# Cross-attention and ternary FFN on one core: the high halves of the FFN's passes as fp16 beside fp32r low halves

## The reference, cut to what matters

```python
x = x + xattn(layernorm(x), ctx)          # softmax(q k^T) v Wo, per batch of 256 rows
n = layernorm(x)                          # no gains
def bitlinear(x, w):                      # w is replaced by sign-like values in {-1, 0, 1}
    scale = clip(mean(abs(w), axis=1), 1e-5)
    tern = clip(round(w / scale), -1, 1)
    return x @ (tern * scale).T
h = bitlinear(n, w_fc) + gate * (n @ v.T @ fast_b.T @ u.T)    # 512 -> 2048, rank 16
r = max(h, 0)
x = x + bitlinear(r * r, w_proj)          # 2048 -> 512
```

## Time and profile before

| what | value |
|---|---|
| median of 3 runs | 780.21 us (779.91 to 780.46) |
| the profiled execution | 779.99 us, its span 778.2 us |
| TensorE busy (PE) | 766.5 us, 98% |
| weight loads (PEld) | 637.6 us, 82%, beside PE |
| VectorE (DVE) | 547.6 us, 70% |
| ScalarE (ACT) | 368.6 us, 47% |
| GpSimd (POOL) | 107.4 us, 14% |
| granted TensorE clock | 1.00 of full speed over the span |

### The profile page before, as it was taken

How to read it: one execution, slowest core, us unless ns; L and a number is a source line. 1 busy time by engine, 2 the same in 40 slices (tenths; PEclk the granted TensorE clock), 3 DMA queues, 4 the chain that set the end, 5 groups by cost and what they waited for, 6 DMA issues and landing times.

```text
span 778.2 us, 10596 instructions
## 1 busy us (share of the span) xinstructions
PE 766.5 (98%) x3767; PEld 637.6 (82%) x3767; DVE 547.6 (70%) x1118; ACT 368.6 (47%) x690; POOL 107.4 (14%) x125
## 2 busy tenths in 40 slices
PE   7999999999999999999999999999999999999997
PEld 4678788888888888888888888888888888888886
DVE  5999766778676777667766786768667686656434
ACT  5998744354434535354434545254542644233332
POOL 3101300100211030110312020210202002100001
PEclk9999999999999999999999999999999999999999
DMA  8743431163115322063214422063212430040101
GB/s 315 248 150 109 63 88 41 21 96 87 56 40 84 58 72 85 13 97 69 81 42 65 65 75 96 1 99 70 90 41 41 75 88 1 1 54 9 47 0 55
DMA packets 180125, 56.20 MB, mean 72 GB/s; under 512 B 167620, under 2 KB 167894, under 8 KB 180072
## 3 DMA queue, kind: packets, MB, share of 16 engines
q1 hardware_dynamic: 149940, 50.79, 26.8%
q10 hardware_dynamic: 30132, 4.73, 3.8%
HBM read 26.92 MB, written 8.39 MB: 45 GB/s over the span
## 4 chain that ended last, share of the span: by engine, by line
PE 97%; DVE 1%; ACT 1%; issue 0%; DMA 0%; DVEq 0%; ACTq 0%
PE H L1357 30%; PE O L1338 29%; PE G L1220 26%; PE H L1363 4%; PE H L1220 1%; PE H L1197 1%; PE H L1204 1%; PE O L1412 1%; PE G L1304 1%; PE O L1378 1%; PE H L1185 1%; PE G L1248 0%; DMA Wq_s<-in_L_xattn_Wq_dram 0%; DVE x2a L1057 0%; PE O L1395 0%
## 5 line engine op out<-in xcount | busy, mean ns | idle before, releaser
L1338 PE MATMUL O<-projT,qbuf 128*128 128x512 f32 x992 | 242.1, 390 | 0.0
L1338 PEld LDWEIGHTS O<-projT,qbuf 128*128 128x128 f32 x992 | 185.0, 188 | 38.2
L779 ACT ACTIVATE rbuf<-H,scf 128x512 f32<-128x512 f32 x128 | 87.5, 684 | 124.9 <-DVE qbuf L1116 75.7
L1357 PE MATMUL H<-even_group,fcT 128*128 128x512 f32 x512 | 127.5, 391 | 0.0
L1357 PE MATMUL H<-odd_group,fcT 128*128 128x512 f32 x512 | 127.3, 391 | 0.0
L1112 DVE TENSOR_TENSOR rbuf<-rbuf 128x512 f32<-128x512 f32 x128 | 91.5, 723 | 45.9 <-ACT rbuf L779 45.9
L787 ACT ACTIVATE qbuf<-rbuf 128x512 fp32r<-128x512 f32 x125 | 78.5, 628 | 89.7 <-PE O L1338 62.7
L1116 DVE TENSOR_TENSOR qbuf<-rbuf,qbuf 128x512 fp32r<-128x512 f32 x125 | 85.9, 688 | 36.5 <-ACT qbuf L787 35.8
L1357 PEld LDWEIGHTS H<-odd_group,fcT 128*128 128x128 f32 x512 | 95.3, 188 | 19.3
L1357 PEld LDWEIGHTS H<-even_group,fcT 128*128 128x128 f32 x512 | 95.1, 188 | 19.2
L1220 PE MATMUL G<-Wvo,tT 128*128 128x512 f32 x270 | 64.7, 389 | 0.0
(11 more groups left out here) (194 smaller groups left out, 989.0 us busy)
## 6 DMA issues: line engine op xcount, KB each, us to landing
xb<-in_x_dram SPq DMA_DIRECT2D x8, 1024.0 KB, 5.1
n_blocks<-n_rows SPq DMA_DIRECT2D x112, 64.0 KB, 2.3
ctxb<-in_ctx_dram SPq DMA_DIRECT2D x8, 768.0 KB, 4.3
n_blocks<-ctxb SPq DMA_DIRECT2D x112, 48.0 KB, 2.2
wring<-in_L_ffn_w_fc_dram SPq DMA_DIRECT2D x16, 256.0 KB, 6.2
wring<-in_L_ffn_w_proj_dram SPq DMA_DIRECT2D x16, 256.0 KB, 2.7
out_dram<-x2a SPq DMA_DIRECT2D x8, 512.0 KB, 2.7
x_blocks<-x_rows SPq DMA_DIRECT2D x56, 64.0 KB, 3.5
```

The source lines that it names most:

```text
L779: nc.scalar.activation(rbuf[:, j % 2, :], banks[f"H{j % 2}"][:, :], ACT.Relu, scale=scf[:, j:j + 1]).then_inc(relu_made, 1)
L1338: mm = pe.matmul(banks[f"O{t}"][:, :], qbuf[:, j % 2, h, t * P:(t + 1) * P], projT[:, j, :], start=(j == 0 and h == HI), stop=(j == NFF - ...
L1357: pe.matmul(banks[f"H{j % 2}"][:, :], fcT[:, k, j * P:(j + 1) * P], xnT[:, h, k, :], start=(k == 0 and h == HI), stop=False)
```

## The change

1. The high halves of the FFN's input and of the squares are fp16 tiles (`hi16_of`, `square_hi`; for the last pieces `late_square_hi`). The weights of their passes are the same ternary tiles, read as bf16 through every second 2-byte element (`fc16`, `pc16`). Low halves, the low-rank pass and the attention stay fp32r.
2. `up` and `down` do the four passes of one half, then the four of the other. They begin with the half of the kind that came last (`latest`): fp16 when the piece before ended with high halves, else fp32r. After a piece of the attention it is the fp32r kind. The low-rank pass goes with the low half. A `down` that begins with low halves waits for `lo:j` at its start, one that begins with high halves waits for `hi:j` there and for `lo:j` four passes later.
3. `L:0` still wants fp32r high halves: GpSimd copies them (`x32:0` to `x32:3`, once in each body, and twice as many half-size copies in the prologue).
4. So that squares fit fp16, the scale of the hidden rows is divided by a power of two that comes from a bound made on the chip in the prologue: GpSimd's `peaks`, `power`, `bound`, `rescale`; VectorE's `widest`, `q:0`, `q:1`, `root`; TensorE's `q:0`, `q:1`.
5. Orders: in BODY_ORDER and LAST_ORDER two `down` follow two `up`; at the start of body 0 `up:0` and `up:1` are cut into `main` and `rank`, with `L:0` behind `main:0`; in BODY_ORDER `xhi3` goes ahead of `nc1+` and `xraw3` ahead of `lo:14`.

```diff
 BODY_ORDER "pe":
-        "up:12 down:9 up:13 down:10 up:14 down:11 up:15 down:12 down:13 "
+        "down:9 up:12 up:13 down:10 down:11 up:14 up:15 down:12 down:13 "
 BODY_ORDER "act":
-        "hi:11 up:12 nc0+ xhi0 up:13 xhi1 xhi2 hi:12 hi:13 up:14 up:15 hi:14 nc1+ nc2+ hi:15 xhi3 nc3+ "
+        "hi:11 up:12 nc0+ xhi0 up:13 xhi1 xhi2 hi:12 hi:13 up:14 up:15 hi:14 xhi3 nc1+ hi:15 nc2+ nc3+ "
 BODY_ORDER "dve":
-        "sq:14 sq:15 lo:14 xraw3 xlo3 lo:15 "
+        "sq:14 sq:15 xraw3 lo:14 xlo3 lo:15 "
 BODY_ORDER and FIRST_ORDER "pool":
-        "residual xs23+ a:0 a:1 a:2 a:3 cs23+ "
+        "residual xs23+ a:0 a:1 a:2 a:3 cs23+ x32:0 x32:1 x32:2 x32:3 "
 LAST_ORDER "pe":
-        "... up:2 down:0 up:3 down:1 up:4 down:2 ... down:9 up:12 down:10 up:13 up:14 up:15 down:11 "
+        "... up:2 up:3 down:0 down:1 up:4 up:5 down:2 down:3 ... down:9 up:12 up:13 down:10 up:14 up:15 down:11 "
 PROLOGUE "pe":
-        "... s:3 ut:0 ut:1 ut:2 turn:22 pT:1 w:0 ... x:3 sprow B.L:0 B.up:0 B.up:1 B.up:2 turn:31 "
+        "... s:3 q:0 ut:0 ut:1 ut:2 turn:22 q:1 pT:1 w:0 ... x:3 sprow B.main:0 B.L:0 B.main:1 B.rank:0 turn:31 B.rank:1 B.up:2 "
 PROLOGUE "dve":
-        "... round:25 pT:0 s:3 abs:31 n2:3 round:26 round:27 pT:1 B.xs01 B.xs23 w:0 ... B.cs23 B.L:0 B.sq:0 round:31 B.lo:0 ..."
+        "... round:25 widest pT:0 s:3 q:0 abs:31 n2:3 round:26 round:27 q:1 pT:1 B.xs01 B.xs23 root w:0 ... B.cs23 round:31 B.L:0 B.sq:0 B.lo:0 ..."
+        fc16 = fcT[:, :, :].bitcast(BF16).rearrange("p k (n h) -> p k n h", h=2)[:, :, :, 1]
+        pc16 = projT[:, :, :].bitcast(BF16).rearrange("p n (d h) -> p n d h", h=2)[:, :, :, 1]
 # GpSimd, a step x32:k of a body
+            pool.wait_ge(xhi_made, KD * b + k + 1)
+            nc.gpsimd.tensor_copy(xhi32(g, k), hi16_of[g % 2][:, k, :]).then_inc(xhi32_made, 1)
 # TensorE
             def down(b, j):
-                pe.wait_ge(sqlo_made, NFF * b + j + 1)
+                pe.wait_ge(sqhi_made, NFF * b + j + 1)
-                for t in range(TILES):
-                    for h in (HI, LO):
-                        mm = pe.matmul(banks[f"O{t}"][:, :], qbuf[:, j % 2, h, t * P:(t + 1) * P], projT[:, j, :],
-                                       start=(j == 0 and h == HI), stop=(j == NFF - 1 and h == LO))
-                mm.then_inc(down_full, 1)
+                halves = order_of_halves()
+                for h in halves:
+                    if h == LO:
+                        pe.wait_ge(sqlo_made, NFF * b + j + 1)
+                    for t in range(TILES):
+                        latest["pass"] = pe.matmul(
+                            banks[f"O{t}"][:, :], squares(b, j)[h][:, t * P:(t + 1) * P], (pc16, projT)[h][:, j, :],
+                            start=(j == 0 and h == halves[0]), stop=(j == NFF - 1 and h == halves[1]))
+                latest["half"] = halves[1]
+                done(down_full)
+            def up_half(b, j, h, start, stop):
+                for k in range(KD):
+                    ternary = (fc16 if h == HI else fcT)[:, k, j * P:(j + 1) * P]
+                    tokens = hi16_of[b % 2][:, k, :] if h == HI else group_of[b % 2][:, LO, k, :]
+                    latest["pass"] = pe.matmul(banks[f"H{j % 2}"][:, :], ternary, tokens,
+                                               start=(start and k == 0), stop=(stop and k == KD - 1))
+                latest["half"] = h
 # a step "up": halves = order_of_halves() if kind == "up" and j > 0 else (HI, LO)
```

More of the change, by code:

```diff
@@ L34 @@
 F32R = mybir.dt.float32r
+I32 = mybir.dt.int32
 BF16 = mybir.dt.bfloat16
@@ L47 @@
 FIRST_LATE = NFF - 3
+CREST = 60.0
 ATTENTION = ([("n1T", t) for t in range(4)] + [("n2T", t) for t in range(4)]
@@ L74, in on_act @@
 def on_act(unit):
-    return unit[0] != "a"
+    return unit[0] not in ("a", "q")
 def n_full(b, unit):
@@ L93, in bank_of @@
 def bank_of(b, unit):
-    n = unit_list(b).index(unit)
+    if unit[0] == "q":
+        return f"{'GH'[unit[1]]}0"
+    n = [u for u in unit_list(b) if u not in RANGE].index(unit)
     if b >= 0:
@@ L383, in mk_xattn_ffn @@
         raw_of[0] = under("even_halves", [P, 2, KD, TOK])
+        hi16_of[0] = under("even_hi16", [P, KD, TOK], FP16)
         even = sb("even_group", [P, 2, KD, TOK], F32R)
@@ L386, in mk_xattn_ffn @@
         rbuf = sb("rbuf", [P, 2, TOK])
-        qbuf = sb("qbuf", [P, 2, 2, TOK], F32R)
+        square_hi = sb("square_hi", [P, 2, TOK], FP16)
+        square_lo = sb("square_lo", [P, 2, TOK], F32R)
+        sb("below_x2b", [P, 512])
         x2b = sb("x2b", [P, TILES, D])
+        peaks = sb("peaks_of_squares", [P, NFF, RK])
+        pair = sb("pair_of_peaks", [P, 2, NFF])
+        power = sb("power_of_FB", [P, KD, 16])
+        widest = sb("widest", [P, 2])
+        crest = sb("crest", [P, 4])
+        bound = sb("bound", [P, 2])
+        root = sb("root", [P, 2])
+        scf2 = sb("scf_of_scaled_squares", [P, NFF])
+        spc2 = sb("spc_of_scaled_squares", [P, KD])
+        fsq = sb("power_of_FB_rows", [P, 1])
         x2 = [x2a, x2b]
@@ L943, in unit @@
                     return
+                if kind == "q":
+                    dve.wait_ge(unit_full, n_full(b, un))
+                    if t == 0:
+                        link(nc.vector.tensor_reduce(crest[0:2, 3:4], bank[0:2, 0:P], AX_X, ALU.max))
+                        nc.vector.tensor_scalar(root[0:2, :], ident[0:2, 0:2], crest[0:2, 3:4], None, ALU.mult
+                                                ).then_inc(unit_dve, 1)
+                    else:
+                        nc.vector.tensor_copy(crest[:, 0:3], bank[:, 0:3]).then_inc(unit_dve, 1)
+                    return
                 if kind == "a":
@@ L1135, in steps @@
                                                 ALU.add, apply_absolute_value=True).then_inc(abs_by_dve, 1)
+                    elif kind == "root":
+                        dve.wait_ge(bound_made, 1)
+                        link(nc.vector.tensor_scalar(root[:, 0:1].bitcast(I32), bound[:, 1:2].bitcast(I32), 0x7F800000, None,
+                                                     ALU.bitwise_and))
+                        nc.vector.reciprocal(root[:, 1:2], root[:, 0:1]).then_inc(root_made, 1)
+                    elif kind == "widest":
+                        dve.wait_ge(peaks_made, 1)
+                        nc.vector.tensor_reduce(widest[:, :], pair[:, :, :], AX_X, ALU.max).then_inc(widest_made, 1)
                     elif kind == "uprep":
@@ L1257, in unit @@
                     else:
-                        pe.wait_ge(xhi_made, KD * b)
-                        products(bank[:, :], [(FB[:, k, :], xnT[:, HI, k, :]) for k in range(KD)], last=False)
+                        products(bank[:, :], highs, last=False)
                         pe.wait_ge(xlo_made, KD * b)
@@ L1325, in turn_free, with order_of_halves, done @@
                     piece_stored(pe, j - 4)
+            latest = {"pass": None, "half": LO}
+            def order_of_halves():
+                return (latest["half"], 1 - latest["half"])
+            def done(full):
+                latest["pass"].then_inc(full, 1)
             def down(b, j):
-                pe.wait_ge(sqlo_made, NFF * b + j + 1)
+                pe.wait_ge(sqhi_made, NFF * b + j + 1)
                 if j == 0:
@@ L1408, in _ @@
             for t in range(TILES):
-                for j in range(NFF - 4, NFF):
-                    pe.wait_ge(sqlo_made, NFF * (NG - 1) + j + 1)
-                    for h in (HI, LO):
-                        mm = pe.matmul(banks[f"O{t}"][:, :], squares(NG - 1, j)[:, h, t * P:(t + 1) * P], projT[:, j, :],
-                                       start=False, stop=(j == NFF - 1 and h == LO))
-                mm.then_inc(down_full, 1)
+                halves = order_of_halves() if t > 0 else (HI, LO)
+                for h in halves:
+                    for j in range(NFF - 4, NFF):
+                        pe.wait_ge((sqhi_made, sqlo_made)[h], NFF * (NG - 1) + j + 1)
+                        latest["pass"] = pe.matmul(
+                            banks[f"O{t}"][:, :], squares(NG - 1, j)[h][:, t * P:(t + 1) * P], (pc16, projT)[h][:, j, :],
+                            start=False, stop=(j == NFF - 1 and h == halves[1]))
+                latest["half"] = halves[1]
+                done(down_full)
 _INS = ['x', 'ctx_768', 'L0_xattn_ln1_g', 'L0_xattn_ln1_b', 'L0_xattn_ln2_g', 'L0_xattn_ln2_b', 'L0_xattn_Wq',
```

166 lines of the change are left out of this document (126 added, 40 removed), and 12 rows, old and new, of the table PROLOGUE.

## The result

| | before | after |
|---|---|---|
| median of the runs | 780.34 us (779.91 to 780.46, 4 runs) | 791.53 us (790.92 to 792.22, 4 runs) |
| ratio | | 1.0146, interval 1.013 to 1.0162 |
| profiled execution, its span | 779.99 us, 778.2 us | 791.44 us, 789.6 us |

The change makes the kernel slower by 11.2 us. The forecast was 780.5 us, its range ended at 788.0: wrong in size and outside the range. The nearest case was rival 3's 791.0 us, which was given 0.07; as will be seen, it holds for one half of its passes only, and the rest of the time comes from elsewhere.

The account below looks back on a forecast made before the run. TensorE, busy for 98% of the span, was taken to bound the kernel. The terms -10.5 + 2.3 + 6.4 + 1.4 + 0.7 = +0.3 us on 779.99 us led to a forecast of 780.5 us, range 774.0 to 788.0.

Parts of the forecast that it names:

- rival 3: The fp16 passes are no faster, as weights at every second element or mixed types cost 10.3 ns: 791.0 us, chance 0.07.
- Part 1: In up and down, 1024 high-half passes become fp16, each 10.3 ns shorter than fp32r: -10.5 us.
- Part 2: On TensorE, 163 changes of kind to fp16 and as many back, 14 ns a pair: +2.3 us.
- Part 3: In bodies 1 to 5, down:9, moved ahead of up:12, waits 1.27 us for lo:9: +6.4 us.
- Parts 4 and 5: Start of body 0: up:2 and up:3 wait for the relu, +1.4 us; prologue: VectorE's steps for the bound, +0.7 us.
- the excursion of 104 ns at 91.64: Kernel before, 91.64 to 93.78 us: fp16 and fp32r passes take 104 ns over due; upper bound on changes, 17.0 us.
- Rival 1: At changes of kind, the fp32r load waits for the fp16 passes, up to 104 ns each: 795.2 us, chance 0.22.
- Rival 2: The wait at down:9 in bodies 1 to 5 doesn't come: 774.1 us, chance 0.15.
- Part 6: Splitting into fp16 on ScalarE and VectorE, and GpSimd's copies in the bodies (widest operation 1.55 us), cost nothing.

Follow-up runs that it names:

- e1: The changed kernel with the high-half passes of down moving packed 2-byte elements of projT in place of every second one (wrong numbers): 786.44 us.
- e2: The changed kernel with the high-half passes of up moving every second 2-byte element in place of the packed fp16 tile (wrong numbers): 796.75 us, a single execution.
- e5: The kernel of e4 with high and low halves alternating pass by pass in every up and down, 128 pairs of changes a body instead of 32: 798.4 us.
- e3: The changed kernel with lo:9 moved right behind lo:8, ahead of sq:10 and cs23+, in VectorE's order of bodies 1 to 6: 785.78 us.
- e4: The kernel of e3 with every up and down beginning with its high halves, 32 pairs of changes a body instead of 21: 785.42 us.
- e6: The kernel of e4 with the start of body 0 in the order before the change: 783.92 us.
- e7: The kernel of e6 without the bound of the squares and all that makes it, the power of two being the constant 1: 783.02 us.
- f3: The kernel of e4 with the whole FFN in 16 bits, packed bf16 weights, no GpSimd copies, and body 0 started in the order before: 757.05 us.
- f1: The kernel of e4 with the FFN in 16 bits, packed bf16 weights and no GpSimd copies, but low-rank tiles and passes in fp32r: 763.74 us.

## Why the prediction was wrong, by its own steps

| step | forecast, us | found, us |
|---|---|---|
| Part 1, fp16 passes | -10.5 | -5.7 (`up`, 512 x 11.2 ns), -0.4 (`down`, 512 x 0.7 ns) |
| Part 2, changes of kind | +2.3 | +2.6 (163 x 16 ns, at the change itself) |
| nothing in the forecast: the fp32r passes behind a change | 0 | +3.7 (0.48 a body, 7.75 bodies' worth) |
| Part 3, `down:9` | +6.4 | +6.8 (5 x 1.36) |
| Parts 4 and 5, start and prologue | +2.1 | +4.3 (3.33 + 0.94 in the table of bodies) |
| sum | +0.3 | +11.3, of 11.45 in the profiled executions |

Of the 11.0 us between the two sums Part 1 holds 4.4, the changes with the passes behind them 4.0, the start 2.2 and `down:9` 0.4. That the measured time lies beside rival 3's 791.0 us is chance: of that rival's 10.5 us only 4.4 came.

**Part 1 failed in one sentence:** "Reading one half of each 4-byte weight takes no more bytes per column than today's read, so I price it at nothing". It is right for weights that are loaded (`up`) and wrong for weights that move (`down`), where the step of 4 bytes costs all of the gain. The bound stood beside it, no faster than fp32r, and rival 3 named the mechanism ("weights at every second element"); but I treated both products alike, though the code shows that `projT` is the moving operand of `down` and `fcT` the loaded one of `up`. e1 and e2 show it: 0.58 us less and 0.57 more in body 6, -5.1 and +5.2 us in all. The estimate of 216.4 ns for a packed pass was good; 215.5 was measured.

**Part 2** was right on the change itself (14 ns forecast, 15 in the records of after), and "Behind a 216 ns pass it is hidden, and I take 0" holds up within some 4 ns. What failed is the step behind it, which took every remaining fp32r pass at today's 226.7 ns. They came out at 224 to 239, so that a pair costs 38 ns in after. The prediction's own rows bear it: the excursion of 104 ns at 91.64 has, behind its first fp32r pass, five more at 228 to 236 ns in the records, but only the first was read, and the rest went into a bound. Rival 1 (104 ns a pair, an fp32r load that begins only when the fp16 passes are through) is refuted as a mechanism: in after the fp32r load starts at 89.48, just as the last of four fp16 passes does (88.82 + 3 x 0.216), and e5 with many times the pairs cost 17 ns for each more. Its size was not so far off: 38 ns lies above the 24 at which it was to decide.

**Part 3 was right** in place, cause and count: five waits for `lo:9` at `down:9`, none in body 6, 1.14 us each for 1.27 forecast. The wait is shorter because TensorE's pieces ahead of it didn't get shorter by 34 ns each; with faster passes it is 1.21 (e1), with slower ones 1.05 (e2). The price in time is larger than the wait, 1.36. e3 removes it with one word moved in VectorE's order. Rival 2 (no wait) is refuted for the change, and e3 shows what it would have been worth.

**Parts 4 and 5.** The waits for the relu were there but at 0.26 + 0.59 instead of 0.5 + 0.9. Missed was the wait of `down:0` for the last weight store, 1.26 us: the prediction named TensorE's bank as what comes late, and did not follow ScalarE's queue behind the later relu (`hi:1`, then the store), nor the slow square beside GpSimd's residual. The three waits make 2.1 us, but the new order costs only 1.5 more than the old one (e4 against e6), since it saves `L:0` a wait of 0.65 for the copies. The bound costs 0.9 (e6 against e7), forecast 0.7. Together 2.4. What is left of the 4.3 can be read in e7, which has the old start and no bound: at the end of its body 0 it is still 1.3 us behind before (86.98 + 88.24 against 85.69 + 88.23). Of these 0.6 are the wait of `L:0` for the copies, and 0.4 are there already at the first passes over `M` (46.42 against 46.04 us, 46.49 in after), ahead of everything that TensorE does anew. Those 0.4 are no work of the change as far as the traces show: executions of the other versions reach the same passes between 46.07 us (f3) and 49.56 (e3). The last 0.3 stays open.

**Part 6 was right.** In a body a copy of GpSimd takes 0.61 to 1.13 us, under the 1.55 by which it was bounded, and in after no `L:0` waits for one. Timeline of GpSimd in after, body 3:

```profile
355.75 0.61 POOL L696 CAST odd_group<-odd_hi 128x512 fp32r<-128x512 f16 x1 [7.42 <-ACT odd_hi L903]
```

**Why the fp32r passes are slow.** It isn't that they are low halves. In body 6 of after a run of 18 attention passes stands behind fp16 passes, and four low halves of `up` stand behind the run:

```profile
681.01 4.48 PE L1331 MATMUL G<-Wvo,tT 128*128 128x512 f32 x18
685.33 1.07 PE L1487 MATMUL H<-even_group,fcT 128*128 128x512 f32 x4
```

By the records the run goes at 418, 235, 233, 236, 224, 231, 236, 228, 233, 231 ns and from there on at 226 or 227, and so do the four low halves: 227, 226, 227, 227. (The 418 holds what the fp16 pass ahead took: it is recorded as 29 ns long up to the next start.) The first ten or so fp32r passes behind fp16 ones are slow, whatever they multiply, and a piece of four or eight ends before that. Of the 0.46 us of body 6 the attention's 512-column runs hold 0.14.

Nor does it take a change of kind. In body 6 of before, all fp32r, a `down` behind passes of 256 columns is slow in the same way, and an `up` behind passes of 512 isn't:

```profile
664.60 2.00 PE L1338 MATMUL O<-projT,qbuf 128*128 128x512 f32 x8
...
674.02 1.98 PE L1357 MATMUL H<-even_group,fcT 128*128 128x512 f32 x8
```

The first has 233, 236, 228, 233, 231, 226, 227, 227 ns by the records, the second 226 or 227 throughout. So fp32r passes of 512 columns come back to 226.7 ns only by and by behind passes that were shorter, fp16 or narrow. That fits the prices of a pair: least where a single fp32r pass stands between the changes (e5, f1), most where a run follows. Open is what makes the first ones slow; no run here varies it alone.

## What to carry to other kernels

When a split operand is stored inside a wider one and read at every second element, ask for each product whether it is loaded or moving: loaded it was free here, moving it cost the whole gain of the narrower type. A stream of passes gains from a narrower type by going over to it whole: half of the passes in fp16 gave nothing that could be measured in an undisturbed body (89.53 us against 89.47), all of them gave 3 us of 89. Price a change of kind by the ten passes behind it, not by the first alone. And after reordering pieces, list for each engine which late result the moved piece now waits for first, and follow the queue behind it: one word in VectorE's order was worth 5.7 us.

## What was not expected of the hardware

- A 512-column pass takes 215.5 ns when 2-byte elements move packed, and 225 to 227 ns when they move at a step of 4 bytes, as much as fp32r (226.7). The step on the loaded side costs nothing: 98 ns a load and 215.5 a pass.
- A change from a 2-byte kind to fp32r and back costs 19 ns together in e5 and 22 to 24 in f1, with one fp32r pass between, and 38 in after, where the next fp32r passes are slow too. The records show it as an fp32r pass that starts 25 to 43 ns behind the fp16 one and lasts long.
- Behind shorter passes, fp16 or of 256 columns, the first five to ten fp32r passes of 512 columns mostly run at 228 to 236 ns and only then at 226.7, in before as in after.
- VectorE's square of 128x512 takes 0.69 us alone and 1.48 or 1.76 us beside GpSimd's residual at the start of body 0.
